# Two mixers moved between the turns of the edge stages of a four-layer graph network, and per-node values spread to edges in bf16 pieces

## What is computed

```python
xn = _layernorm(x)                                   # layer 1 (the second)
x = x + rgcn(xn) + softmax_mix(xn)
#   rgcn: sum over edges of w_e * (xn[src] @ weight[type]) / max(count(type, dst), 1)
#         + xn @ root + bias
#   softmax_mix: n = rmsnorm(xn) * g_pre; q, k, v = split(n @ w_qkv)
#         q = softmax(q, over the 32 features of a head) * scale
#         k = softmax(k, over all nodes and 4 memory rows)
#         out = rmsnorm((q @ (k^T v)) @ w_out + b_out) * g_out ; result out + xn
xn = _layernorm(x)                                   # layer 2
x = x + gin(xn) + head_norm_mix(xn)
#   gin: segment_sum(edge_weight * xn[src], dst), then two batch-normed products
#   head_norm_mix: d = t - mean, per head of 32; k, v = w * d / (std + eps) + b
#         kv = k^T v / N per head; result t @ kv + t
xn = _layernorm(x)                                   # layer 3
x = x + graph_attention(xn) + squared_mix(xn)        # e = exp(-leaky_relu(s[src] + t[dst]))
```

## Time and profile before

| | us |
|---|---|
| median of 3 runs | 7497.59 (7496.27 to 7501.97) |
| the profiled execution's own time | 7498.07 |
| its span | 7496.4 |
| PE, DVE, ACT, POOL busy | 4494.6, 3397.3, 1888.4, 3731.6 |
| gathers of g1e on POOL, first to last start | 3254.1 to 3889.0 |
| gathers of g2e | 4580.7 to 5204.0 |
| gathers of g3e | 6297.0 to 7043.5 |

### The profile page before, as it was taken

The page is one execution under the profiler, slowest core; times in us unless marked ns, Lnnn a source line. Parts: engine busy times, 40 slices in busy tenths (PEclk is TensorE's granted clock), DMA queues, the critical chain, the costliest instruction groups (busy, mean ns, idle before and its releaser), DMA issues. The chain is left out here.

```text
span 7496.4 us, 74035 instructions
## 1 busy us (share of the span) xinstructions
PE 4494.6 (60%) x18035; PEld 3311.2 (44%) x18035; DVE 3397.3 (45%) x8025; ACT 1888.4 (25%) x4800; POOL 3731.6 (50%) x3581
## 2 busy tenths in 40 slices
PE   0160666666664791978864763555438965997528
PEld 0030444444443571356653652333237853665415
DVE  6840677777777314343336124332471115442361
ACT  0000555555554120023331110000102212442201
POOL 0776777777774363047750554775004433774300
PEclk9985777777776796977766886776769987996659
DMA  0020444444442472334360322336005642332400
GB/s 37 10 57 11 125 122 123 122 123 121 121 125 68 138 213 69 127 97 105 103 80 5 101 74 84 105 105 82 14 7 184 187 138 80 104 104 62 46 21 17
DMA packets 390998, 677.71 MB, mean 90 GB/s; under 512 B 127989, under 2 KB 257180, under 8 KB 387124
## 3 DMA queue, kind: packets, MB, share of 16 engines
q0 software_dynamic: 188992, 431.92, 23.7%
q1 hardware_dynamic: 201638, 241.74, 10.0%
HBM read 591.29 MB, written 81.90 MB: 90 GB/s over the span
## 5 line engine op out<-in xcount | busy, mean ns | idle before, releaser
L1209 POOL DMA_INDIRECT g0e_got<-g_table,g0e_rc x496 | 594.8, 1199 | 293.5 <-issue 157.0
L986 POOL DMA_INDIRECT g1e_got<-g_table,g1e_rc x496 | 485.1, 978 | 477.6 <-DMA g1e_rc<-rec_dst 326.9
L986 POOL DMA_INDIRECT g3e_got<-g_table,g3e_rc x496 | 490.0, 988 | 349.9 <-issue 142.4
L1211 POOL DMA_INDIRECT g0e_keyed<-g_keys,g0e_rc x496 | 572.2, 1154 | 166.6 <-issue 166.6
L986 POOL DMA_INDIRECT g2e_got<-g_table,g2e_rc x496 | 473.5, 955 | 261.1 <-issue 147.1
L1051 PE MATMUL g2e_pa<-g2e_got,g2e_placew 128*125 128x256 f32 x992 | 361.1, 529 | 323.4 <-issue 217.8
L257 POOL DMA_INDIRECT rec_dst<-bydst_rc,bydst_sloti x391 | 394.1, 1008 | 294.3 <-DVEq L449 175.4
L1273 PE MATMUL g0e_pt<-g0e_new,g0e_placet 125*128 125x8 f32 x992 | 211.0, 341 | 490.7 <-DVEq L1343 490.7
L1247 ACT ACTIVATE g0e_spaced<-g0e_spread 125x512 bf16<-125x512 f32 x992 | 499.1, 627 | 21.8 <-PE g0e_spread L1283 19.7
L2153 PE MATMUL f_p<-f_w2s,f_hid 128*128 128x256 f32 (+1 forms) x2176 | 493.1, 383 | 12.7 <-ACT f_hid L2173 1.7
L2142 PE MATMUL f_p<-f_xt,f_w1s 128*128 128x256 f32 (+1 forms) x2176 | 491.3, 383 | 14.4 <-DMA f_b2s<-in_L_ffn_b 8.9
(11 more groups left out here) (609 smaller groups left out, 8559.2 us busy)
## 6 DMA issues: line engine op xcount, KB each, us to landing
f_w1s<-in_L_ffn_W SPq DMA_DIRECT2D x32, 1024.0 KB, 5.7
f_w2s<-in_L_ffn_W SPq DMA_DIRECT2D x32, 1024.0 KB, 7.6
g_table<-g1t_out SPq DMA_DIRECT2D x25, 1000.0 KB
f_w1s<-in_L_ffn_w SPq DMA_DIRECT2D x40, 512.0 KB
f_w2s<-in_L_ffn_w SPq DMA_DIRECT2D x40, 512.0 KB
f_results<-f_y SPq DMA_DIRECT2D x72, 256.0 KB, 2.2
f_b2s<-in_L_ffn_b SPq DMA_DIRECT2D x80, 128.0 KB, 6.9
f_rows<-XN SPq DMA_DIRECT2D x3, 3125.0 KB
```

Source lines behind the costliest of these rows:

```text
L986: pool.indirect_dma_start(got[:, g % GOTS, j, :], None, table, bass.IndirectOffsetOnAxis(rc[:, g * GT + j, idx:idx + 1], 0))\
L1209: pool.indirect_dma_start(got[:, s, j, :], None, table, bass.IndirectOffsetOnAxis(rc[:, sl, j, R_IDX:R_IDX + 1], 0)).then_inc(got_in[s], 16)
L1211: pool.indirect_dma_start(keyed[:, s, j, :], None, keys, bass.IndirectOffsetOnAxis(rc[:, sl, j, R_KEY:R_KEY + 1], 0)).then_inc(got_in[s], 16)
```

## The change

Two classes after the pattern of `SquaredMixer` take the place of two mixers: `SoftmaxMixer`, the side of g1e, which also holds the product with `root` and its bias, and `HeadNormMixer`, the side of g2e. g1e adds straight into `X`, without `g1_acc`, its memset and `add_stage`. In `edge_stage`, `spread` is split once, at the stage's start, into three bf16 pieces that add up to it; `placet` is bf16, one bf16 matmul brings all three pieces to an edge, and DVE adds them up.

```diff
@@ edge_stage
-            placet = sb("placet", [P, 4, GT, 128])
+            placet = sb("placet", [P, 4, GT, 128], BF16)
+            pieces = sb("pieces", [P, NT, 3, sw], BF16)
+            rest = sb("rest", [P, NT, sw])
...
-                        last = pe.matmul(pq[g % turns][:, j, 0:sw], placet[:, g % 4, j, :], spread[:, ds(at * sw, sw)],
-                                         start=True, stop=True)
+                        last = pe.matmul(pq[g % turns][:, j, 0:3 * sw], placet[:, g % 4, j, :],
+                                         pieces[:, ds(at, 1), :, :].rearrange("p a n e -> p (a n e)"), start=True, stop=True)
...
+            if spreads:
+                whole = spread.rearrange("p (t e) -> p t e", e=sw)
+                dve.tensor_copy(rest[:, :, :], whole)
+                dve.drain()
+                for piece in range(3):
+                    dve.tensor_copy(pieces[:, :, piece, :], rest[:, :, :])
+                    dve.drain()
+                    if piece < 2:
+                        dve.tensor_tensor(rest[:, :, :], rest[:, :, :], pieces[:, :, piece, :], ALU.subtract)
+                        dve.drain()
+                dve.sem_inc(split, 1)
...
-                        dve.tensor_tensor(coef[:, g % 4, :], pq[g % turns][:, 0:GT, 0], got[:, g % GOTS, :, wide - 1], ALU.add)
+                        dve.tensor_reduce(coef2[:, g % 4, :], pq[g % turns][:, 0:GT, 0:3], AX.X, ALU.add)
+                        dve.drain()
+                        dve.tensor_tensor(coef[:, g % 4, :], coef2[:, g % 4, :], got[:, g % GOTS, :, wide - 1], ALU.add)
@@ relation_graph_layer
-        rows_stage(nc, R, "g1root", w[:, :, :], D, finish_root,
...
-        edge_stage(nc, R, "g1e", "relation", by_dst, acc[:, :], D, table, idx=R_ROW, spread=R.inv_count[:, :])
-        add_stage(nc, [(R.X, acc)])
+        edge_stage(nc, R, "g1e", "relation", by_dst, R.X[:, :], D, table, idx=R_ROW, spread=R.inv_count[:, :],
+                   side=SoftmaxMixer(nc, R, ctx, a), clear=False)
@@ isomorphism_graph_layer
-        edge_stage(nc, R, "g2e", "weight", by_dst, acc[:, :], D, table)
+        with ExitStack() as inner:
+            edge_stage(nc, R, "g2e", "weight", by_dst, acc[:, :], D, table, side=HeadNormMixer(nc, R, inner, a))
@@ program
-            softmax_mixer(nc, R, "m1", a["L1_mix_w_qkv"], a["L1_mix_w_out"], a["L1_mix_b_out"], a["L1_mix_g_pre"],
-                          a["L1_mix_mem_kv"], a["L1_mix_g_out"])
...
-            head_norm_mixer(nc, R, a)
```

More of the change, by code:

```diff
@@ L952, in edge_stage @@
         coef2 = sb("coef2", [128, 4, GT])
+        expd = sb("expd", [128, 4, GT])
         if spreads:
             pt = [ctx.enter_context(nc.psum_tensor(f"{name}_pt{k}", [P, 1024], BF16)) for k in range(turns)]
-            pq = [ctx.enter_context(nc.psum_tensor(f"{name}_pq{k}", [128, 64, 8], F32)) for k in range(turns)]
+            pq = [ctx.enter_context(nc.psum_tensor(f"{name}_pq{k}", [128, 16, 32], F32)) for k in range(turns)]
         pa = [ctx.enter_context(nc.psum_tensor(f"{name}_pa{k}", [P, 512], F32)) for k in range(adds)]
@@ L958, in edge_stage @@
         got_in = [sem(f"got_in{k}") for k in range(GOTS)]
-        names = ("placed", "weighed", "turned", "evacuated", "spreaded", "logit", "expd", "summed", "added")
-        placed, weighed, turned, evacuated, spreaded, logit, expd, summed, added = (sem(n) for n in names)
+        names = ("split", "placed", "weighed", "turned", "evacuated", "spreaded", "logit", "summed", "added")
+        split, placed, weighed, turned, evacuated, spreaded, logit, summed, added = (sem(n) for n in names)
         block = ctx.enter_context(nc.Block())
@@ L998, in _ @@
                     if mode == "gat":
-                        act.activation(coef2[:, g % 4, :], coef[:, g % 4, :], ACT.Exp, scale=-1.0)
+                        act.activation(expd[:, g % 4, :], coef[:, g % 4, :], ACT.Exp, scale=-1.0)
                         act.drain()
-                        weights = coef2
+                        weights = expd
                     if g >= 3:
@@ L1032, in _ @@
                     pe.wait_ge(evacuated, g + 1)
+                    if g == 0:
+                        pe.wait_ge(split, 1)
                     if g >= turns:
@@ L1097, in _ @@
                         dve.drain()
-                        dve.tensor_tensor(small[:, g % 2, :, :], pq[g % turns][:, 0:GT, :], rel[:, g % 2, :, :], ALU.mult)
+                        dve.tensor_tensor(small[:, g % 2, :, :, :], pq[g % turns][:, 0:GT, 0:24].rearrange("p j (n e) -> p j n e", e=8),
+                                          rel[:, g % 2, :, :].rearrange("p j (a e) -> p j a e", a=1).broadcast_to([128, GT, 3, 8]),
+                                          ALU.mult)
                         dve.drain()
-                        dve.tensor_reduce(coef2[:, g % 4, :], small[:, g % 2, :, :], AX.X, ALU.add)
+                        dve.tensor_reduce(coef2[:, g % 4, :], small[:, g % 2, :, :, :].rearrange("p j n e -> p j (n e)"), AX.X, ALU.add)
                         dve.drain()
```

476 lines of the change are left out of this document (386 added, 90 removed).

## The result

| | before | after |
|---|---|---|
| median, us | 7497.26 (4 runs) | 7154.29 (4 runs, 7151.87 to 7158.86) |
| ratio | | 0.9544, 95% interval 0.9533 to 0.9556 |
| span of the profiled execution | 7496.4 | 7150.0 |
| PE, DVE, ACT, POOL busy | 4494.6, 3397.3, 1888.4, 3731.6 | 4265.2, 3457.6, 1917.7, 3729.1 |

The change saves 343 us; 287 were forecast, with a range that holds the result, though the forecast's own bounds (7165 to 7295) do not. The time is within 3 us of the first rival's, *the cover holds*, 7152.

The account below looks back on a forecast made before the run. The prediction took POOL's gathers to bound g1e and g2e, with DVE becoming the bound in g1e's mixer turns. Layer 1, layer 2 and g3e gave 147 + 120 + 20 = 287 off 7498.07: 7211 us, range 7145 to 7305.

Parts of the forecast that it names:

- the cover holds: Rival: g1e's mixer turns keep POOL's pace and only single steps cost, 202 + 124 + 20 less, 7152 us; chance 0.22.
- The stages removed, 204 and 124 us: Layer 1 around g1e loses 203.9 us of serial work, layer 2 the mixer's stages of 124.4 us.
- g1e grows by 57: Taking on the mixer lengthens g1e by 80 - 20 - 3 = 57 us; the forecast's own bounds 30 to 110.
- The allowance for PE at half speed: In g1e's 50 tile turns, 0.4 us a turn on average for stretches in which PE falls behind, making 6.0.
- The 19 us for the output turns: g1e's last 25 turns take 5.9 us against POOL's 5.13: 25 x 0.77 = 19 us more.
- The 17 us of early squares and single steps: In g1e, ACT's early squares, DVE's scaling of weights and single steps waiting for PE: 17 us together, an estimate.
- The 20 us for POOL's lead: In g1e POOL may run six groups ahead, normally some two, so 20 us of the growth is not lost.
- g2e grows by 4: With the mixer, g2e's DVE turns average 5.0 us against POOL's 5.04; 4 us put, layer 2 120 us less.
- g3e's output turns, 20 less: The bf16 pieces shorten the round trip of DVE and PE in g3e's output turns: 25 x 0.8 = 20 us less.
- PE at half clock throughout: Rival: PE stays at half clock in g1e, which grows by the upper bound, g2e by some 15: 7325 us; chance 0.12.
- POOL held up by DVE: Rival: each added microsecond of DVE holds POOL, g1e losing 154 us and g2e 130: 7431 us; chance 0.04.
- The slower rival: DVE waits for PE within the same turn in g1e, 97 turns of 9.97 us in place of 5.13: 7601; chance 0.04.

Follow-up runs that it names:

- run 6: The changed kernel with two more sums of 256 columns on DVE in each of g1e's 50 tile turns: 7196.60 us, ratio 0.9598.
- run 10: The changed kernel with the per-node values spread in fp32 again in place of bf16 pieces: 7199.42 us, ratio 0.9606.
- run 9: The changed kernel with room for 4 fetched groups in g1e in place of 6: 7174.29 us, ratio 0.9575.
- run 5: The changed kernel itself, without an edit, as a yardstick on another chip: 7155.78 us, ratio 0.9551.
- Runs 8: The kernel before with the bf16 pieces alone, both mixers staying stages of their own: 7469.88 us, ratio 0.9965.
- run 7: The changed kernel with DVE's tile part of g1e's mixer one turn earlier, waiting for PE inside its own turn: 7392.49 us, ratio 0.9861.
- run 4: The changed kernel with DVE's output part of g3e's mixer one turn later, where the kernel before takes 8011.6 us: 7606.1 us, ratio 0.9495.
- run 12: The changed kernel with 8 rooms in g1e, g2e's and g3e's mixer outputs one turn later, empty records spread over the table: 7563.81 us (before 7981.7), ratio 0.9478.

## Why the prediction was right, and where it was off

**The stages removed, 204 and 124 us:** right, as far as the landmarks show. They were serial, and nothing took their place.

**g1e grows by 57:** this is the term that was mis-sized; the stage took 677.4 us, 8 more than its 669.2, where the forecast's own lower bound was 30 more. Its parts fared differently.
- The turn of DVE, 5.55 us, was right (5.5), and so was the claim that it is above POOL's pace; run 6 shows that DVE binds once the rooms are full.
- The allowance for PE at half speed was wrong, and it was the largest error: 0.4 us a turn, 20 us, in the tile turns and 0.3, 8 us, in the output turns. The clock itself was forecast well: it was 0.89 and 0.86, where the prediction looked for 0.75 to 0.9. What failed is the step from half speed to a longer turn. A pair of turns with PE at half speed for a third of the time took the same 11.0 us, and all that half speed and everything else added was 0.07 a turn (5.57 for 5.5). (The prediction's own count of PE's turn is loose: it puts the mixer's part at 1.07 and at 1.4, and the total at 4.1. PE's turn is under DVE's by either.)
- The 19 us for the output turns were counted in full. The text said that turns without a mixer would catch up after them; it missed that the 12 key turns and the steps around them had already emptied the lag, from 31 to 12 us, so the rise to 24 cost nothing.
- The 17 us of early squares and single steps became 3: nothing held POOL at the squares, and the single steps held it once, for 3.0 us, since they came while the rooms were full. The early turns are not free, though: they set the lag with which the tile turns start, and run 10, which starts 5 us higher, loses 5.
- The 20 us for POOL's lead was right (14.4 to 31, 17 us), and run 9 prices it: two rooms less, 11 us more.

By the trace DVE's sums are 5.57 us apart from group 4 to 42 and POOL's groups 5.10: an excess of 50 x 0.47 = 24 us, less 17 of lag, 7. POOL's stops of over 1 us, beyond the usual 0.3, add up to 10 for the tile turns and 3 for the single steps; the first gather, no longer beside a memset, takes 1.29 us for 3.87, 3 less. That makes 10, with 8 or 9 measured. So *the cover holds* gave the right time, and not for the reason that it named: it held because of the rooms, not because DVE had time left. And that the total lies in the stated range is in part luck: the range had been widened to take in that rival, and of the forecast's own signs the gathers' span in g1e (some 690 us, measured 643.7) and POOL's waits of tens of microseconds in the tile turns (19.8 in the whole stage) did not come.

**g2e grows by 4:** 4.2 by the landmarks (124.4 less the 120.2 saved). **g3e's output turns, 20 less:** 23 in the stage, 19 by run 5's trace of the same kernel. Three of the sums of output tiles, a pair of turns:

```profile
6502.08 0.48 DVE L912 SCALAR_TENSOR_TENSOR X<-m_pa,m_s,X 125x256 f32<-125x256 f32 x1 [4.30 <-PE m_pa L765]
6511.11 0.48 DVE L912 SCALAR_TENSOR_TENSOR X<-m_pt,m_s,X 125x256 f32<-125x256 f32 x1 [5.48 <-PE m_pt L765]
6519.05 0.48 DVE L912 SCALAR_TENSOR_TENSOR X<-m_pa,m_s,X 125x256 f32<-125x256 f32 x1 [4.39 <-PE m_pa L765]
```

The turn went from 9.52 us on average to 8.54; the 9.97 of the earlier trace rows was a long one, and the cut of 0.8 a turn was nearly right at 1.0. Runs 8 and 10 put the pieces' share there at 16.5 and 23.

**The rivals.** PE at half clock throughout did not come (0.89). POOL held up by DVE did not either: DVE is busy 65% of the tile stretch, and the gathers' median stays 946 ns, and in run 6, with 100 more sums of two SBUF tensors, it is still 946. The Trainium skill (SBUF, "Who interferes with whom"), which the prediction had cited, lets such sums pass beside GpSimd's writes; these traces agree. The slower rival was turned aside by the one turn of lag, and run 7 shows it real: 4.7 us a turn.

**What the text missed** is that the turns of g3e, which it took as given, were the same fault: one `yield` there was worth 61 to 65 us. And the last groups, at 6.7 us with the transfers late, stand in both kernels alike (DMA share 0.98 in g1e's last groups before), so they did not disturb the sum.

## What to carry to other kernels

Compare each engine's turn with the pace of the pipeline, and then ask how much lag the buffers allow and when it is paid back: here 50 turns at 9% over the pace make 24 us; six rooms hid 17 of them, and from then on every microsecond counted. A consumer woven into a loop should use a product one turn after it is issued; using it in the same turn cost 4.7 us a turn in g1e, a round trip of all engines. And padding should not point at one address: with the empty records spread, the work behind g3e's last gather took 12 us for 24.

## What was not expected of the hardware

- Gathers in which all 128 rows are the same row of HBM: packets of 4128 bytes took 795 ns on average for 241 with rows apart (runs 4 and 12, end of g3e), and 796 for 220 at the end of g1e with 4096 bytes.
- A memset on DVE holds a gather on POOL until it is over. In the earlier trace rows the first gather of g1e starts at 3254.05 under the memset that ends at 3257.00, and ends itself at 3257.92. The same 0.9 us behind the memset's end stands in all 30 such cases (g2e and g3e of every kernel, g1e where it has a memset); the 12 first gathers of g1e without one take 1.28 or 1.29 us. So the row from which the prediction took that DVE can hold POOL was read rightly, but the mixer's instructions leave the gathers' median at 946 ns.
- The chips are of two kinds for this kernel: 7497 to 7498 us and 7982 to 8012 us for the same program. On the slower kind POOL stands some 30 times in g2e, nearly 3 us about every 16 gathers (89.6 us in all in run 12), and the gathers' transfers pause too (19 pauses of over 1.5 us in 400 us of g2e in run 4, none in the changed kernel's trace); packets themselves are no longer (231 ns in g1e of run 4, 242 in the changed kernel). The profile names no plausible releaser (a record transfer long over, or none). What stops them is open.
